# Constant products of TensorE that nobody reads, placed in the waits of a graph network's dense stage and of its woven convolutions

## What is computed

```python
edge_index = jnp.stack([src, dst])
h = jnp.maximum(_layernorm(x, axis=-1), 0.0)
x = x + _L0_gnn_ref(h, edge_index, edge_attr_32, ...)   # gated messages, update, layernorm
h = jnp.maximum(_layernorm(x, axis=-1), 0.0)
x = x + _L1_gnn_ref(h, ..., edge_attr_96, src, dst)     # z = [h, m]; relu(z @ Wu1 + bu1) @ Wu2 + bu2
h = jnp.maximum(_layernorm(x, axis=-1), 0.0)
x = x + _L2_gnn_ref(h, edge_index, L2_gnn_W, L2_gnn_b)  # mean of x[src] @ W + b over the edges of a node
h = jnp.maximum(_layernorm(x, axis=-1), 0.0)
x = x + _L3_gnn_ref(h, src, dst, ...)                   # three graph convolutions, relu after each
```

## Time and profile before

| | |
|---|---|
| time, median of 3 runs | 6821.34 us (6820.54 to 6821.72) |
| profiled execution, its own time | 6816.94 us |
| its span, first to last instruction | 6815.1 us |
| TensorE busy in the span | 4880.8 us (72%) |
| VectorE, ScalarE, GpSimd busy | 62%, 51%, 50% |
| mean granted TensorE clock | 0.693 of full |

### The profile page before, as it was taken

The page is one execution under the profiler, slowest core; times in us unless marked ns, Lnnn a source line. Parts: engine busy times, 40 slices in busy tenths (PEclk is TensorE's granted clock), DMA queues, the critical chain, the costliest instruction groups (busy, mean ns, idle before and its releaser), DMA issues. The chain is left out here.

```text
span 6815.1 us, 112075 instructions
## 1 busy us (share of the span) xinstructions
PE 4880.8 (72%) x20595; PEld 3298.6 (48%) x20595; DVE 4231.1 (62%) x13898; ACT 3492.7 (51%) x8824; POOL 3381.2 (50%) x3542
## 2 busy tenths in 40 slices
PE   5767888888887999979999777777767777222222
PEld 2225555555554444446666466656655655222221
DVE  5665555555556888877777688878864444222222
ACT  6984444444446999955555455545543333111110
POOL 0005444444445444434344366656655553777777
PEclk9995555555557999989999876666665555555555
DMA  0002222222223344345555477656556666433332
GB/s 15 0 0 75 73 73 73 74 73 73 73 74 83 94 95 95 88 106 143 142 140 141 129 194 187 186 139 159 154 135 123 130 127 118 69 60 68 64 71 57
DMA packets 1144575, 677.18 MB, mean 99 GB/s; under 512 B 898138, under 2 KB 1096550, under 8 KB 1144461
## 3 DMA queue, kind: packets, MB, share of 16 engines
q1 hardware_dynamic: 1031500, 526.97, 28.4%
q0 software_dynamic: 112960, 148.99, 13.3%
HBM read 445.59 MB, written 232.52 MB: 100 GB/s over the span
## 5 line engine op out<-in xcount | busy, mean ns | idle before, releaser
L717 POOL DMA_INDIRECT xs<-t,idx x1176 | 1110.1, 944 | 978.1 <-DMA idx<-at 583.3
L1182 PE MATMUL bank<-ident,msg 128*96 128x128 f32 (+1 forms) x1568 | 389.4, 397 | 921.4 <-ACT msg L985 721.7
L717 POOL DMA_INDIRECT xs<-c,idx x784 | 748.9, 955 | 519.2 <-DMA idx<-at 290.1
L1189 PE MATMUL bank<-w,aggT 96*128 96x96 f32 (+1 forms) x3136 | 679.2, 388 | 294.1 <-DVE aggT L1474 293.1
L1189 PEld LDWEIGHTS bank<-w,aggT 96*128 96x128 f32 (+1 forms) x3136 | 626.5, 296 | 375.5 <-issue 267.5
L1474 DVE TENSOR_TENSOR_SCAN aggT<-goes,aggT,bank 96x512 f32<-96x512 f16 (+1 forms) x490 | 621.2, 1268 | 263.1 <-PE bank L1135 112.0
L1182 PEld LDWEIGHTS bank<-ident,msg 128*96 128x96 f32 (+1 forms) x1568 | 275.3, 201 | 971.4 <-ACT msg L985 592.0
L717 POOL DMA_INDIRECT got<-info_d,idx x392 | 370.7, 946 | 694.8 <-DMA found<-got 590.4
L985 ACT ACTIVATE msg<-xs,now 128x96 f32<-128x96 f32 x784 | 225.4, 365 | 905.1 <-DMA xs<-c,idx 604.5
L1048 PEld LDWEIGHTS bank<-uw,u 97*128 97x128 f32 x1568 | 419.3, 327 | 479.5 <-ACT u L873 326.4
L1048 PE MATMUL bank<-uw,u 97*128 97x96 f32 x1568 | 518.0, 434 | 161.1 <-ACT u L873 161.1
(11 more groups left out here) (228 smaller groups left out, 11129.3 us busy)
## 6 DMA issues: line engine op xcount, KB each, us to landing
t<-xn SPq DMA_DIRECT2D x294, 192.0 KB, 2.3
xd<-t SPq DMA_DIRECT2D x294, 192.0 KB, 3.6
goes<-goes_d SPq DMA_DIRECT2D x392, 128.0 KB
xd<-in_x_dram SPq DMA_DIRECT2D x196, 192.0 KB, 2.4
t<-xo SPq DMA_DIRECT2D x196, 192.0 KB
hd<-t SPq DMA_DIRECT2D x196, 192.0 KB
hs<-t SPq DMA_DIRECT2D x196, 192.0 KB
out_dram<-oo SPq DMA_DIRECT2D x196, 192.0 KB
```

Of the source, the lines that this page charges most:

```text
L717: nc.gpsimd.indirect_dma_start(out=into, out_offset=None, in_=table, in_offset=bass.IndirectOffsetOnAxis(ap=indices, axis=0)).then_inc(don ...
L1182: ins = nc.tensor.transpose(bank[g.at(2)][0:m, c * P:(c + 1) * P], msg[:, g.at(2), c, 0:m], ident[:])
L1189: ins = nc.tensor.matmul(tok(bank[2 + g.at(2)], m)[:, c, :], aggT[0:m, g.at(3), c * P:(c + 1) * P], w2[:] if k == 0 else w3[:, k - 1, :], ...
```

## The change

It adds a helper `keep_busy(columns)`: one float32 product of `before` with the first columns of `cols`, 384 of them (`BUSY`), into bank 7. It waits for nothing, signals nothing, and nothing reads its output. In the dense stage two such products stand in TensorE's order of each step, one ahead of `tr1` and one ahead of `z1`. In the three woven convolutions each step begins with one of them, or with three in each third step, the one without a step of the node pass. To free bank 7, `node_z` and `node_relu` use bank 5 alone, and both engines' orders in the node pass are swapped: ScalarE runs `node_relu` ahead of `node_evac`, TensorE runs `node_out` ahead of `node_z`.

```diff
--- before.py
+++ after.py
@@ -26,6 +26,7 @@
 NODE_PER = 4
 NODE_STEPS = 66
 WOVEN_FIRST = 18
+BUSY = 384
 HI, LO = 128, 784
 SIDE = LO // 2
 NEAREST = 1.5 * 2 ** 23
@@ -881,7 +882,7 @@
             def node_relu(g):
                 need(act, nd["z1"], g.j + 1)
                 need(act, nd["u1"], g.j - 1)
-                nc.scalar.activation(v1[0:D, g.at(2), :], bank[5 + 2 * g.at(2)][0:D, :], ACT.Relu, bias=bias[:, 4:5])\
+                nc.scalar.activation(v1[0:D, g.at(2), :], bank[5][0:D, :], ACT.Relu, bias=bias[:, 4:5])\
                     .then_inc(nd["g1"].sem, 1)
 
             act.wait_ge(const_step, 1)
@@ -987,7 +988,7 @@
                     ins.then_inc(ph["h"].sem, 1)
 
                 if k < 3:
-                    woven(act, k, [(rows_in, 3 if k < 2 else 0)], [(node_evac, 3), (node_relu, 4), (node_norm, 2)])
+                    woven(act, k, [(rows_in, 3 if k < 2 else 0)], [(node_relu, 4), (node_evac, 3), (node_norm, 2)])
                 else:
                     pipelined(act, EG, [(rows_in, 0)])
 
@@ -1028,6 +1029,14 @@
                 nc.tensor.matmul(into, w, x, start=True, stop=True).then_inc(done.sem, 1)
 
 
+            steady = cols[:].rearrange("p k t -> p (k t)")
+
+            def keep_busy(columns):
+                nc.tensor.matmul(bank[7][:, 0:columns], before[:], steady[:, 0:columns], start=True, stop=True)
+
+            def dense_busy(g):
+                keep_busy(BUSY)
+
             def tr1(g):
                 need(pe, dn["norm"], g.j + 1)
                 need(pe, dn["r1"], g.j)
@@ -1058,8 +1067,8 @@
 
             def node_z(g):
                 need(pe, nd["r1"], g.j + 1)
-                need(pe, nd["g1"], g.j - 1)
-                products(bank[5 + 2 * g.at(2)][0:D, :], wu1[:, 0, :], hsT[0:D, g.at(2), :], nd["z1"])
+                need(pe, nd["g1"], g.j)
+                products(bank[5][0:D, :], wu1[:, 0, :], hsT[0:D, g.at(2), :], nd["z1"])
 
             def node_out(g):
                 need(pe, nd["g1"], g.j + 1)
@@ -1073,7 +1082,7 @@
             pe.wait_ge(table_step, 7)
             pe.wait_ge(const_step, 1)
             pe.wait_ge(idx_step, 1)
-            pipelined(pe, NG, [(out1, 1), (tr1, 0), (z1, 0)])
+            pipelined(pe, NG, [(out1, 1), (dense_busy, 0), (tr1, 0), (dense_busy, 0), (z1, 0)])
 
             need(pe, dn["norm_y"], NG)
             for ph in (e0, e1):
@@ -1182,6 +1191,10 @@
                         ins = nc.tensor.transpose(bank[g.at(2)][0:m, c * P:(c + 1) * P], msg[:, g.at(2), c, 0:m], ident[:])
                     ins.then_inc(ph["seg"].sem, 1)
 
+                def conv_busy(g):
+                    for _ in range(1 if g.c % 3 < 2 else 3):
+                        keep_busy(BUSY)
+
                 def apply_w(g):
                     need(pe, ph["agg"], g.j + 1)
                     need(pe, ph["xr"], g.j - 1)
@@ -1192,7 +1205,8 @@
 
                 stages = [(turn_rows, 3), (apply_w, 4)] if k < 2 else [(turn_rows, 0), (apply_w, 1)]
                 if k < 3:
-                    woven(pe, k, stages, [(node_z, 3), (node_out, 4), (node_turn, 2)])
+                    stages = [(conv_busy, 0)] + stages
+                    woven(pe, k, stages, [(node_out, 4), (node_z, 3), (node_turn, 2)])
                 else:
                     pipelined(pe, EG, stages)
                 need(pe, ph["xr"], EG)
```

## The result

The changed kernel takes 6291.28 us (median; 6285.74 to 6302.26) against 6820.94 us for the kernel before beside it (6820.11 to 6821.72): a ratio of 0.9225, 95% interval 0.921 to 0.9241. That is inside the forecast's range and 95 us above its value.

A forecast was written before the change was run, and what follows sets the result against it. A dense-stage chain of TensorE and ScalarE hand-overs, TensorE at half clock, was taken as the bound. Dense -495 and convolutions -20, -20, -90 sum to -625, from 6816.94 to 6192, plus 4.4 for the median: 6196 us; range 6110 to 6440.

The forecast's parts named there:

- The chain of hand-overs: Dense stage before: TensorE and ScalarE alternate through `out1`, `tr1`, evacuation, `z1` and gelu without overlap, 8.06 us a round.
- the first product lies wholly on the path: Dense stage: the added product between `out1` and `tr1` delays `tr1` by its full 0.64 us at full clock.
- order of what comes next: Dense stage, next late after the 5.50 us chain: ScalarE at 5.29, VectorE at 5.21, GpSimd at 4.94 us a round.
- The round of 5.50: Dense stage at full clock: 8.06 - 3.20 + 0.64 = 5.50 us a round, the chain still the longest.
- The second product's cover: Dense stage: the product behind `tr1` runs while ScalarE evacuates and costs nothing, with 0.2 us to spare; uncovered, 0.64.
- The -20: First and second convolution: 20 us less each, placed near VectorE's 37.5 us wait for `apply_w`; bounds -37 to +135.
- 6.22 us in one go in every three steps at half clock, 3.1 less at full: Third convolution: TensorE's stretch on the chain; with 0.5 us from the swapped order, best -119 us, taken as -90.
- the 3.5 that was named as a sign: Third convolution: TensorE's 6.2 us in a row on the chain should fall to some 3.5 us.
- (a): Dense stage: GpSimd's gathers become the bound, 5.77 us a round, time about 6250 us; chance 14%.
- (b): Dense stage: the clock swings; about 6730 us at a mean of 0.68, near 6420 at 0.90; chance 10%.
- (c): The clock does not rise: dense round 9.72 us, convolutions pay 135 us each, about 7550 us; chance 6%.
- (d): Dense stage as forecast, but the convolutions' products cost what they do at half clock: about 6730 us; chance 4%.

The follow-up runs named there:

- behind_z1: The changed kernel with the dense stage's first added product moved from ahead of `tr1` to behind `z1`: 6201.6 us.
- swap_only: The changed kernel without any added product, keeping the swapped node orders and the single bank for `node_z`: 6780.0 us.
- sync_only: The kernel before, with only SyncE's loads of `goes` and `now` issued two steps earlier in the third convolution: 6691.8 us.
- one_ahead_z1: The changed kernel with only the dense product ahead of `z1` kept, and no products in the convolutions: 6265.5 us.
- quarter_rows: The changed kernel without the convolutions' products, its dense products fed with 32 of the 128 rows: 7280.6 us.
- conv_only: The changed kernel without the dense stage's added products, keeping the convolutions' products and the swapped orders: 6754.6 us.
- sync_ahead_bare: behind_z1 without products in the convolutions, and with SyncE's loads of `goes` and `now` two steps earlier in the third convolution: 6110.6 us.
- sync_ahead: behind_z1 with the convolutions' products between `turn_rows` and `apply_w`, and SyncE's `goes` and `now` loads two steps earlier in the third convolution: 6110.8 us.

## Why the prediction was right, and where it was off

| term | forecast | measured in the profiled executions |
|---|---|---|
| dense stage | -495 | 195 x (5.769 - 8.107) = -456 |
| first convolution | -20 | 555.7 - 569.6 = -14 |
| second convolution | -20 | 547.1 - 564.4 = -17 |
| third convolution | -90 | 672.1 - 706.5 = -34 |
| all else | 0 | +5 (edge phases +4, last convolution +1) |
| sum | -625 | -516, against 6302.26 - 6816.94 = -515 |

**What bounds the kernel: right.** The chain of hand-overs read from one round of before is the chain after, step by step, and its clock rose within the first rounds. behind_z1 confirms the step that the first product lies wholly on the path: moving it gave 0.48 us a round, and would have given more had VectorE not come next at 5.23, where the earlier trace rows had put its work at 5.21. The forecast's order of what comes next was wrong: it had ScalarE at 5.29 ahead of VectorE, and ScalarE's loop in behind_z1 is 5.11.

**The round of 5.50: 0.19 too low**, 37 us over the stage and nearly the whole miss of 39. By term, forecast and measured: `out1` 1.74 and 1.86, the added product 0.64 and 0.68, `tr1` 0.64 and 0.60, `z1` 1.02 and 1.10; the hand-overs fit to 0.01. The failed step is taking durations from the earlier trace rows, where products follow products without a break. After a pause the first pair of `out1` costs 0.30 from start to start, the following ones 0.22; that is 0.08 of the 0.12. The second product's cover was said to have 0.2 us to spare; it had none: it ends 1.25 us after the start of `tr1` where the estimate had 1.12, and the tile is there at 1.28 instead of 1.33. It still cost nothing.

**First and second convolution: right in size, wrong in cause.** The -20 was to come from VectorE's wait for a faster `apply_w`. That wait went up (37.5 to 43.6). swap_only shows where the gain is from: -10 and -18 with no product added. The forecast valued the swap in the third convolution alone. Nor did the products cost anything there: with TensorE idle in each step for the rows of ScalarE, they found their cover.

**Third convolution: the term of the sum that was mis-sized most**, -34 for -90. The step that failed is "6.22 us in one go in every three steps at half clock, 3.1 less at full", from the earlier trace rows, taken as a saving. That stretch, `apply_w` to `node_turn`, did get shorter, from a mean of 6.09 to 4.53 us over the 64 in each trace, though not to the 3.5 that was named as a sign. TensorE's part of the chain shrank by some 100 us of the listed lines, but 41 of what was left was the added products, nearly all groups of three begun at half clock; the products were allowed for (best -119, taken -90), their sitting on the chain was not. And I didn't ask what is late next in this stage, as I did in the dense one: the loads behind SyncE's waits. sync_only shows that their place was already the bound of the kernel before. The loads of `now` and `goes` are on that chain of before too, with 135 us; I read its largest entries, TensorE's, and not what released them.

**The rivals.** (a) The mean round is 5.77, the very number that this rival gave, and the time is near its 6250; by the time alone the two could not be told apart. The trace and behind_z1 tell them: GpSimd's wait for `found` is still there, 2.2 us each, and with the same gathers the round fell to 5.29. Its price was wrong: it added the store's landing to GpSimd's work, but GpSimd gathers other rows meanwhile. In behind_z1 a store into `found` issues at 1005.44, a gather of source rows runs from 1006.25 to 1007.19, and the gather that waits for the store starts at 1008.57. (b) did not happen with two products; one_ahead_z1 shows it is near, at 0.95. (c) did not happen; quarter_rows shows that such a kernel is slower, but its products are dearer than those of the change, and by rows at half clock of 128-row products the price of (c) was about right, 9.6 against 9.72. (d) is refuted by conv_only: the convolutions' products give 25, they cost nothing. Why the clock still fell twice for 3.4 us in the dense stage, and why about half of its rounds take 0.07 to 0.15 longer than 5.69, stays open. The longer ones come three in a row in every six, and their time lies in the hand-overs into and out of the gelu, 0.12 and 0.13 us instead of 0.04 and 0.05.

**A version that beats both:** sync_ahead_bare, 6110.6 us, a ratio of 0.8956 (0.8941 to 0.8971), which needs no product in the convolutions. sync_ahead measures the same.

## What to carry to other kernels

When one engine's time on a chain shrinks, follow the chain round once more before counting the saving: what releases the next link, and which in-order queue (here SyncE's loads behind somebody else's store) takes the place. Put filler work where the engine waits for a result of its own chain, not ahead of work that is ready; the same product cost 0.48 us a round in one place and nothing in the other. Durations for a sum are best read from rows with the same neighbours, for the first product after a pause is dearer than one in a row.

## What the runs showed of the hardware that I had not expected

A float32 product of 384 columns fed with 32 rows takes longer than one fed with 128 rows, both at half clock: 1.57 us from start to start in quarter_rows, 1.28 in one_ahead_z1. And it leaves the granted clock at 0.50 with TensorE listed busy for 92%, where 128-row products, at 85%, had 1.00: a busy share read from a trace is no forecast of the clock.
